# A graph network on one core: loops of register-addressed units, and the same units written out with constants

## The reference, cut to what matters

```python
def rgcn(x, W, root, bias):                 # ew: the edge weights scaled to 0..1
    xj = x[src]
    m = 0
    for r in range(4):
        m = m + (edge_type == r)[:, None] * (xj @ W[r])
    return segment_sum(m * ew[:, None], dst) + x @ root + bias

h = maximum(layernorm(x), 0)
h = maximum(rgcn(h, W1, root1, b1), 0)
x = x + rgcn(h, W2, root2, b2)
h = maximum(layernorm(x), 0)
x = x + segment_sum(edge_weight[:, None] * h[src], dst) @ W.T + b
```

## Time and profile before

| what | value |
|---|---|
| time, median of 3 runs (range) | 7167.74 us (7164.68 to 7173.25) |
| the profiled execution | 7208.98 us, span 7207.2 us |
| granted PE clock, mean over the span | 0.576 |
| POOL busy | 4439.8 us (62%) |
| PE matmul / weight load busy | 2694.0 / 2503.1 us |
| DVE / ACT busy | 1721.1 / 434.2 us |
| POOL waiting for DVE's index copies | 1279.9 us |
| HBM traffic | 389 MB in DMA packets, 54 GB/s |

### The profile page before, as it was taken

How to read it: one execution, slowest core, us unless ns; L and a number is a source line. 1 busy time by engine, 2 the same in 40 slices (tenths; PEclk the granted TensorE clock), 3 DMA queues, 4 the chain that set the end, 5 groups by cost and what they waited for, 6 DMA issues and landing times.

```text
span 7207.2 us, 52919 instructions
## 1 busy us (share of the span) xinstructions
PE 2694.0 (37%) x11399; PEld 2503.1 (35%) x11399; DVE 1721.1 (24%) x7377; ACT 434.2 (6%) x1186; POOL 4439.8 (62%) x4697
## 2 busy tenths in 40 slices
PE   1444444444444433333333333333333333333333
PEld 1444343443443433332333333333333333333333
DVE  4222222222222222222222222222212222112221
ACT  3100000000000000000000000000000000000000
POOL 4656566566565556666666666665666666666665
PEclk7677677776776765555555555555555555555555
DMA  4222222222222211111211111211121111112111
GB/s 124 56 55 57 56 59 58 56 57 58 55 59 55 56 50 50 50 50 49 52 50 50 50 50 50 52 50 46 49 51 51 50 50 49 50 51 51 50 50 47
DMA packets 282516, 389.08 MB, mean 54 GB/s; under 512 B 86987, under 2 KB 194904, under 8 KB 282472
## 3 DMA queue, kind: packets, MB, share of 16 engines
q0 software_dynamic: 150048, 307.60, 16.9%
q1 hardware_dynamic: 132424, 80.99, 3.8%
HBM read 336.91 MB, written 51.34 MB: 54 GB/s over the span
## 4 chain that ended last, share of the span: by engine, by line
another core or an unknown queue 45%; issue 18%; DVEq 12%; DVE 11%; DMA 7%; PE 4%; ACT 1%; SPq 0%; POOL 0%; ACTq 0%; POOLq 0%
DMA x_rows<-x 7%; DVE win L1004 5%; DVEq L1004 4%; PE bank L702 2%; DVE win L979 2%; DVE acc L916 2%; DVEq L979 1%; DVEq L908 1%; DVEq L178 1%; DVEq L916 1%; DVEq L165 1%; DVEq L930 1%; DVEq L161 1%; PE bank L637 1%
## 5 line engine op out<-in xcount | busy, mean ns | idle before, releaser
L367 POOL DMA_INDIRECT rows<-table,idx x4625 | 4376.7, 946 | 2718.7 <-issue 1407.4
L730 PE MATMUL bank<-win,rows 128*128 128x48 f32 x6252 | 1444.9, 383 | 2250.2 <-issue 2195.7
L730 PEld LDWEIGHTS bank<-win,rows 128*128 128x128 f32 x6252 | 1447.0, 323 | 2255.3 <-issue 2200.3
L916 DVE TENSOR_TENSOR acc<-acc,bank 128x48 f32 x1173 | 236.8, 202 | 4257.8 <-remote 3829.6
L702 PE MATMUL bank<-win,rows 128*128 128x192 f32 x3126 | 721.6, 384 | 556.4 <-issue 251.9
L702 PEld LDWEIGHTS bank<-win,rows 128*128 128x128 f32 x3126 | 635.6, 230 | 604.3 <-issue 334.3
L979 DVE TENSOR_SCALAR win<-iota,key,sw_col 128x192 f32<-128x192 f32 x1563 | 510.6, 388 | 79.7 <-issue 78.4
L1004 DVE TENSOR_SCALAR win<-iota,rel,sw_col 128x48 f32<-128x48 f32 x1563 | 395.7, 329 | 204.8 <-issue 204.2
L1004 DVE TENSOR_SCALAR win<-iota,rel,w_col 128x48 f32<-128x48 f32 x1563 | 387.9, 327 | 150.5 <-issue 150.5
L674 PE MATMUL bank<-ident,tile_T 128*128 128x128 f32 x98 | 45.8, 469 | 717.5 <-issue 686.7
L644 PE MATMUL bank<-ident,h_rows 128*128 128x128 f32 x98 | 36.9, 377 | 731.1 <-issue 683.4
(11 more groups left out here) (99 smaller groups left out, 1010.2 us busy)
## 6 DMA issues: line engine op xcount, KB each, us to landing
rows<-table,idx POOLq DMA_INDIRECT x4625
table<-st SPq DMA_DIRECT2D x98, 256.0 KB
table<-st SPq DMA_DIRECT2D x98, 64.0 KB
x<-st SPq DMA_DIRECT2D x98, 64.0 KB
x_rows<-x SPq DMA_DIRECT2D x98, 64.0 KB
x_rows<-in_x_dram SPq DMA_DIRECT2D x97, 64.0 KB
h_rows<-table SPq DMA_DIRECT2D x97, 64.0 KB
out_dram<-st SPq DMA_DIRECT2D x97, 64.0 KB
```

The lines of the kernel that those rows point to most:

```text
L367: eng.indirect_dma_start(out=rows[:, slot, :], out_offset=None, in_=table[:, :], in_offset=bass.IndirectOffsetOnAxis(ap=idx[:, slot:slot + ...
L730: ins = eng.matmul(agg_ps[v][:, q * W:(q + 1) * W], rows[:, slot, :], window[:, slot, :], start=(k == 0), stop=(k == n - 1))
L916: eng.tensor_tensor(a, a, sums_ps, ALU.add).then_inc(s_acc, 1)
```

## The change

The unit functions are now called from a Python loop over all 98 units, so that unit numbers, addresses and wait values are constants on every engine. SP's three loops over tiles are written out as well. The holds stay only where the number is a register, and POOL's hold in `gather_unit` is gone. The register that holds a group's first node stays, as it is data. The loops of `general` stay.

```diff
@@ -160,25 +160,19 @@
                 return
             eng.wait_ge(s, v)
 
-        def hold(eng):
-
-            eng.sem_inc(s_hold)
+        def hold(eng, at=None):
+
+            if not isinstance(at, int):
+                eng.sem_inc(s_hold)
 
         def first(b, n):
 
             return isinstance(b, int) and b < n
 
-        def units(eng, unit, whole=True):
-
-            def body(i, n):
-                for v in range(n):
-                    unit(i, v)
-            if whole:
-                body(0, RING)
-            with eng.Fori(1, NI - 2) as i:
-                body(i, RING)
-            body(NI - 2, RING)
-            body(NI - 1, last_units)
+        def units(unit, first_unit=0):
+
+            for u in range(first_unit, NU):
+                unit(u // RING, u % RING)
 
         def tiles(eng, tile):
 
@@ -314,11 +308,7 @@
                     load_x(t + XR, v)
                     load_h(t + XR, v)
 
-            whole = (NT - XR) // XR
-            with eng.Fori(0, whole) as i:
-                for v in range(XR):
-                    tile1_out(i * XR + v, v, True)
-            for t in range(whole * XR, NT):
+            for t in range(NT):
                 tile1_out(t, t % XR, t < NT - XR)
 
             def tile2_out(t, s, i):
@@ -326,7 +316,8 @@
                 eng.dma_start(table2[bass.ds(t * P, P), :], st[:, s, 0:D]).then_inc(s_stored[s], 16)
                 eng.wait_ge(s_fin_d, t + 1)
                 eng.dma_start(x2[bass.ds(t * P, P), :], st[:, s, D:2 * D]).then_inc(s_stored[s], 16)
-            tiles(eng, tile2_out)
+            for t in range(NT):
+                tile2_out(t, t % 2, t // 2)
 
             def load_x2(t, s):
                 eng.dma_start(x_rows[:, s, :], x2[bass.ds(t * P, P), :]).then_inc(s_load[s], 16)
@@ -343,11 +334,8 @@
                 if more:
                     load_x2(t + 2, s)
 
-            with eng.Fori(0, NT // 2 - 1) as i:
-                for v in range(2):
-                    tile_out(i * 2 + v, v, True)
-            for t in range(NT - 2, NT):
-                tile_out(t, t % 2, False)
+            for t in range(NT):
+                tile_out(t, t % 2, t < NT - 2)
             for s in range(2):
                 eng.wait_ge(s_stored[s], stored_by(2, NT // 2))
 
@@ -372,7 +360,6 @@
 
                 u = i * RING + v
                 eng.wait_ge(s_idx, u + (r * NU + 1))
-                hold(eng)
                 for k in range(chunks_of(u)):
                     gather(table, v * UC + k, s_row[v * UC + k])
 
@@ -394,7 +381,7 @@
 
             def fast(r):
                 table_ready(r)
-                units(eng, lambda i, v: gather_unit(gathered[r], r, i, v), whole=r > 0)
+                units(lambda i, v: gather_unit(gathered[r], r, i, v), first_unit=0 if r else RING)
 
             def general(r):
                 table_ready(r)
@@ -478,7 +465,7 @@
             def prep(r, t, s):
 
                 wait(eng, s_fin, t + (r * NT - 1))
-                hold(eng)
+                hold(eng, t)
                 if r == 0:
                     eng.activation(tile_T[:, s, :], columns(t), ACT.Relu, bias=b1s[:, 0:1]).then_inc(s_prep, 1)
                 else:
@@ -531,7 +518,7 @@
                             eng.wait_ge(s_acc, u * UG)
                             eng.wait_ge(s_own0_add, u - 1)
                             prep(0, u - 2, v % 2)
-                units(eng, unit)
+                units(unit)
                 sums_out(NU - 1, NU - 1, 0, 2)
                 sums_out(NU - 1, NU - 1, 1, NG - (NU - 1) * UG - 2)
                 finish0(NT - 3, (NT - 3) % 2, (NT - 3) // 2)
@@ -794,12 +781,12 @@
 
             def mean_and_var(e, p, sources):
 
-                hold(eng)
+                hold(eng, e)
                 for k, rows_k in enumerate(sources):
                     ins = eng.bn_stats(stats[0:rows_k.shape[0], p, k, :], rows_k)
                 ins.then_inc(s_stats, 1)
                 eng.wait_ge(s_stats, e + 1)
-                hold(eng)
+                hold(eng, e)
                 for k, rows_k in enumerate(sources):
                     n = rows_k.shape[0]
                     ins = eng.bn_aggr(mv[0:n, p, k, :], stats[0:n, p, k, :])
```

## The result

The changed kernel took 7060.68 us (median of 4 runs, 7049.97 to 7073.38); the kernel before took 7170.49 beside it (4 runs). The ratio is 0.9844, 95% interval 0.9828 to 0.986: 110 us, or 1.56%, faster. The forecast was 6975 us, in a range of 6700 to 7240. The sign was right; a gain of 194 us was forecast and 110 came. The way was not the one that was forecast.

The account below looks back on a forecast made before the run. GpSimd's gather cadence (5861 us) and 1280 us of index waits, blamed on late TensorE and VectorE, were taken as the bound. 7167.7 less 194 for VectorE's and TensorE's instructions, all else 0, gave 6975 us; range 6700 to 7240.

Parts of the forecast that it names:

- What bounds the kernel: GpSimd's gathers at 1.25 us each, 5861 us, plus 1280 us waiting for index copies because TensorE and VectorE are late.
- the chain: Profile's chain of waits over two units of round 1: 14 VectorE register or branch pieces, 0.70 us each or twice that, then TensorE.
- Part (1): GpSimd's loop branch, register operations and per-unit increment between gathers: taken as 0, at most 9 us.
- Part (2): VectorE's register operations: some 24 of about 30 go per looped unit, each a step in slow stretches; 194 us together with TensorE's.
- Part (3): TensorE's register operations and wait values: some 5 of about 73 instructions per unit go; 76 us if counted alone.
- Part (4): SyncE loses two register operations per store, ScalarE a few per unit; neither is in the cycle's chain, so 0.
- Part (5): Longer written-out code on every engine: 308 instruction packets, 264 more; between 0 and 372 us, taken as 0.
- rival D: Slower: code packets stop late TensorE or VectorE by 1.41 us each, +178 us, 7346 us; chance 0.17.
- rival B: Little: only TensorE's instructions matter, 76 us, 7092 us; chance 0.15.
- the forecast's own range: The span given to the forecast itself, without its rivals: 6900 to 7060 us; chance 0.42.
- C: Nothing: what is used up before slow stretches isn't counted in register operations; 7168 us, chance 0.11.
- By fewer pauses and not by shorter ones: Sign of a right forecast: GpSimd's waits on VectorE's index copy fall from 1280 to about 1085 us through fewer pauses.

Follow-up runs that it names:

- mix_waits: Changed kernel with GpSimd's increment behind the wait back in round 1, and no VectorE index copies in round 2; 7036.96 us, ratio 0.9803 to the kernel before.
- pe_alone: Kernel before with only TensorE's units written out, the other engines' loops kept; 7207.30 us, ratio 0.9999 to the kernel before.
- the four runs: Kernel before with VectorE, TensorE or the other three engines written out alone, and pe_pad; one chip, ratios 0.9934, 0.9999, 0.9881, 0.9818.
- pe_pad: Changed kernel with one empty semaphore increment behind each of a unit's 16 chunks on TensorE; 7078.23 us, ratio 0.9818 to the kernel before.
- half_mm: Changed kernel with every second chunk's matmul left out in rounds 1 and 2; 5920.45 us, ratio 1.0 on a chip without slow steps.
- narrow_rows: Changed kernel gathering 64 features a row in place of 128; 5923.15 us, ratio 1.0003 on a chip without slow steps.
- direct_half: Changed kernel without index copies in all rounds, every second chunk's matmul left out in round 2; 5918.58 us, ratio 0.9997, chip without slow steps.

## Why the prediction was right and where it was wrong

**What bounds the kernel: half right.** The gather stream and the waits for indices were the two things, and the cadence stayed. Wrong was that the wait "says that TensorE (PE) and DVE are late". The unit that POOL waited for had long been computed. What was late is its release, which VectorE got only after POOL had stopped. VectorE's steps, which the chain showed, went with the change, and the release came as late as before. I had read the chain's step from VectorE to TensorE as work that must be done, without counting whose unit TensorE was at.

**Part (1) failed.** "All of it lies between two gathers", worth 0 and at most 9 us, holds for the increment only where the wait doesn't stall. It was priced like an instruction of its own, at some 0.045 us, and put at nothing because the 0.30 us between gathers hide that. At a stalled wait nothing hides it, and the wait that it takes from the gather made the way 0.54 us longer at some 150 pauses. With SyncE and ScalarE written out too it measured 85 us; mix_waits shows POOL's part, 0.51 us a pause, by itself.

**Part (2), taken with (3) at 194 us, was mis-sized.** VectorE's steps did go as forecast. (What it calls increments at L161 are register operations that work out values of waits; its count of 24 stays the same.) L991 has no register operations, and the chain's share on DVE's sequencer fell from 12% to 1%. But the pauses' number didn't follow: 47 in round 1 before and after. VectorE's written-out code gave 0.36 us a pause, 51 us, mostly because fewer instructions stand between its wait and the copy: a register operation and the loop's wait value ahead of the first add, and the copy's address behind it.

**Part (3)** was taken as part of that sum, with 76 us as its own bound; pe_alone measured 0.0 ± 0.1%. **Part (4)** is not told apart from POOL's share beyond the 0.51 us. **Part (5)**, nothing, was right: 227 packets came where 308 were reckoned, and rival D fell, as no engine written out alone made the kernel slower. The rule of the Trainium skill that was named there ("Runtime: NRT & Kernel Launch", instruction fetch mechanics) agrees with that: 2.64 MB of code were fetched in place of 0.49, and TensorE written out alone measured a ratio of 0.9999.

**The forecast and its rivals.** By time the result lies between the forecast and rival B (7092), at the upper end of the forecast's own range. That it lies there is luck in part: on the chip of the four runs 85 of some 137 us came from the engines that were put at nothing, and the part that was to bring 194 brought 51. By its picture it is B or C: a pause at every second unit as now, DVE's pieces gone from the chain, TensorE's slow matmuls in their place. But it is not B's reason. "By fewer pauses and not by shorter ones" came out the other way. The parts add up to 1.86%, as pe_pad's 1.82% does on their chip; the changed kernel's 1.56% is from another chip. In its round 2 the pauses came irregularly, from 2 to 9 us (the first of all was 10), where the kernel before has 7.2 us at nearly each; whether that or the chip makes the difference isn't settled.

**What stays open.** Why a release waits for the gathers to stop on some chips, and why instructions step there; half_mm, narrow_rows and direct_half were to tell and met other chips. Nor is it told apart whether the release waits for the gathers to stop or for TensorE to come through its slow matmuls, as both end in the same pause. Whether the taking of a profile has a part in it, no run here tells. Since POOL runs four units ahead and two releases come in one pause, a longer ring might make pauses rarer; that wasn't tried.

## What to carry to other kernels

Ask of a wait not only who is named, but when the work that it waits for had ended: count units from the producer's last instruction to the consumer's first. In this kernel an instruction between a wait and the first useful one was free only while the wait didn't stall; where it stalled, each such instruction was on the path, once per stall, and on GpSimd for thirty times its own duration. And a gain that lives on stalls is worth what the stalls are: here 1.6% on one chip, 1.8% on a second, and nothing that can be measured on others.

## What was unexpected of the hardware

- An increment of a semaphore between a wait and an indirect DMA on GpSimd costs some 0.5 us when the wait stalls (0.27 us from the copy's end to the gather without it, 0.78 to 0.81 with it), though it runs for 17 ns.
- The same kernel takes 7170 to 7210 us on some chips and 5920 on others, with the same gather cadence of 1.25 us on all.
- On the former, the sums of every second unit in round 1 reach VectorE 32 to 33 us after TensorE's last matmul, and that is some 5.7 us after the gathers stop; on the latter each unit's do after 0.52 us, while gathers stream.
- 16 empty instructions more a unit on TensorE, beside some 67 matmuls and weight loads in rounds 1 and 2, had no cost clear of the noise (1.82% under the kernel before, with the parts at 1.86%).
